# Edges as one transfer, K and V low halves on VectorE, three graph groups per key and value tile and 25 in the query stage, early query weight loads

## The reference, cut to what matters

```python
xn = layernorm(x)
# graph part: 41250 edges, W is 1024 x 1024, sparse, summed where edges repeat
W = zeros(1024, 1024).at[src, dst].add(edge_weight)        # indices over 1023 fall out
g = xn @ W.T + bias
# linear attention, 16 heads of 64
q, k, v = split(xn @ W_qkv)
q, k = relu(rmsnorm(q, qn_w)), relu(rmsnorm(k, kn_w))
kv = einsum('bhnd,bhne->bhde', k, v)
out = einsum('bhnd,bhde->bhne', q, kv) / (q . sum(k) + eps)
x = x + g + out @ W_out + b_out
# mixture of experts: 8 experts, the 2 best for each token
t = rmsnorm(layernorm(x)) * norm_scale
logits = t @ gate_w + gate_b
x = x + sum over the top 2 of softmax(top_v) * (swiglu(t @ w1[e] + b1[e]) @ w2[e] + b2[e])
```

## Time and profile before

| | |
|---|---|
| median of three runs | 1087.6 us |
| the profiled execution | 1086.58 us |
| its span in the profile | 1084.7 us |
| mean granted TensorE clock | 0.948 |
| busy: PE, DVE, ACT, POOL | 948.2, 731.1, 305.3, 186.7 us |

### The profile page before, as it was taken

The page is one execution under the profiler, slowest core; times in us unless marked ns, Lnnn a source line. Parts: engine busy times, 40 slices in busy tenths (PEclk is TensorE's granted clock), DMA queues, the critical chain, the costliest instruction groups (busy, mean ns, idle before and its releaser), DMA issues.

```text
span 1084.7 us, 16241 instructions
## 1 busy us (share of the span) xinstructions
PE 948.2 (87%) x5425; PEld 589.6 (54%) x5426; DVE 731.1 (67%) x1213; ACT 305.3 (28%) x520; POOL 186.7 (17%) x217
## 2 busy tenths in 40 slices
PE   3589899888899599999999999997828999999992
PEld 2346566666566366545656666665615445455551
DVE  4646888999888599715787778765264555555551
ACT  3525333233333111423212222222102333233321
POOL 1210000000000000000334333322201333333321
PEclk9789899999999699999999999998858999999997
DMA  8512566555455601395115555555618997977553
GB/s 255 187 59 78 174 191 197 185 181 159 143 169 173 215 21 40 85 290 170 40 39 145 156 164 170 173 160 168 214 47 300 326 264 192 312 198 192 119 100 58
DMA packets 90410, 176.49 MB, mean 163 GB/s; under 512 B 25235, under 2 KB 40537, under 8 KB 90337
## 3 DMA queue, kind: packets, MB, share of 16 engines
q1 hardware_dynamic: 82577, 147.40, 42.6%
q0 software_dynamic: 7776, 28.32, 11.7%
HBM read 113.54 MB, written 62.67 MB: 162 GB/s over the span
## 4 chain that ended last, share of the span: by engine, by line
PE 35%; DVE 31%; DMA 14%; ACT 6%; issue 5%; POOL 4%; SPq 3%; DVEq 1%; POOLq 0%; ACTq 0%
PE windows L1066 9%; PE bank L943 8%; DMA arena<-t_dram,arena 6%; DMA arena<-in_w_flat 5%; PE bank L1084 4%; DVE arena L1476 4%; DVE arena L1483 3%; DVE arena L1630 3%; PE bank L966 2%; PE bank L790 2%; PE bank L1057 2%; PE bank L972 2%; POOL arena L687 2%; DVE arena L1463 2%; DVE arena L1461 2%
## 5 line engine op out<-in xcount | busy, mean ns | idle before, releaser
L790 PE MATMUL bank<-arena 128*125 128x512 f16 x960 | 222.5, 390 | 31.7 <-POOL arena L656 18.4
L790 PEld LDWEIGHTS bank<-arena 128*125 128x125 f16 x960 | 132.6, 141 | 109.4 <-issue 27.7
L1066 PE MATMUL windows<-arena 128*128 x648 | 148.8, 379 | 0.0
L943 PE MATMUL bank<-arena 128*128 128x416 f16 (+1 forms) x576 | 110.0, 348 | 9.4 <-DMA arena<-split_dram 9.4
L966 PE MATMUL bank<-arena 128*125 128x512 f16 x432 | 99.2, 387 | 8.3 <-DVE arena L1666 6.8
L1066 PEld LDWEIGHTS windows<-arena 128*128 128x128 f16 x648 | 63.4, 98 | 65.1 <-issue 0.5
L972 PE MATMUL bank<-arena 128*125 128x512 f16 x432 | 95.8, 379 | 0.0
L943 PEld LDWEIGHTS bank<-arena 128*128 128x128 f16 x576 | 56.3, 99 | 56.1 <-DMA arena<-split_dram 10.0
L966 PEld LDWEIGHTS bank<-arena 128*125 128x125 f16 x432 | 60.1, 140 | 43.8 <-DVE arena L1666 7.2
L972 PEld LDWEIGHTS bank<-arena 128*125 128x125 f16 x432 | 59.0, 137 | 33.4
L1084 PE MATMUL bank<-arena 128*128 x324 | 74.3, 379 | 2.2 <-DVE arena L1838 2.2
(11 more groups left out here) (243 smaller groups left out, 1453.5 us busy)
## 6 DMA issues: line engine op xcount, KB each, us to landing
arena<-split_dram SPq DMA_DIRECT2D x56, 512.0 KB, 7.0
arena<-in_w_flat SPq DMA_DIRECT2D x44, 512.0 KB, 4.7
split_dram<-arena SPq DMA_DIRECT2D x88, 256.0 KB, 2.7
arena<-in_w_flat SPq DMA_DIRECT2D x40, 256.0 KB, 3.3
split_dram<-arena SPq DMA_DIRECT2D x80, 128.0 KB, 2.3
arena<-in_x SPq DMA_DIRECT2D x20, 448.0 KB
arena<-in_w_qkv SPq DMA_DIRECT2D x8, 1024.0 KB, 9.5
t_dram<-arena SPq DMA_DIRECT2D x10, 448.0 KB
```

Of the source, the lines that this page charges most:

```text
L790: mm = pe.matmul(bank[b][0:TT, :], xt[:, l, k, tok(i)], wkv[:, r, k, c0:c0 + 512], start=(k == 0 and n == 0), stop=(k == KT - 1 and n == 2))
L943: mm = pe.matmul(bank[u % 3][:, 0:n], wq[h][:, l, k, :], xt[:, r, k, a:a + n], start=(k == 0 and c == 0), stop=(k == KT - 1 and c == 2))
L1066: mm = pe.matmul(bank[6][:, :], rowT[s][:, l, k, :], arena16[:, bass.ds(off + (r * KT + k) * 512, 512)], start=(k == 0 and c == 0), stop=( ...
```

## The change

- **Edges.** The host lays `src`, `dst`, `edge_weight` (padded) and the two preceding `dst` of each row side by side, and one transfer loads all. POOL's four memsets and the semaphore ahead of them go. On SP, three weight parts now stand ahead of x of tile 1, and the edges behind it.
- **Low halves of the K and V weights.** All eight on DVE; the second ACT pass for parts 3, 5, 7 goes. Instructions of the start are put in another order on ACT and DVE, `window_picks` behind `v_half(0, ...)`.
- **Halves.** Tile 1 takes six, tiles 2 to 7 five, tiles 8 and 9 four (before: four in tile 1, five in 2 to 9).
- **Groups.** Three a tile (`KV_GROUPS` = 24): the fourth, behind `kv_unit(i, 1, 1536)` on PE and `v_half(i, 1)` on DVE, goes. The query stage has 25, on units 0 to 14, and the splits start at unit 15 (`FIRST_SPLIT`, before 11).
- **Query weights.** `load_wq(0, 0)` is issued at the end of tile 7, (0, 1) ahead of the store of the last half; (2, 1) and (3, 0) stand ahead of the writes of `w_acc`. The last `kv_sums` stands behind query unit 0.
- **Mix.** The quarters per tile are 6, 5, 5, 5, 5, 5, 5, 4 in place of 5, 5, 5, 5, 6, 6, 4, 4, and in tiles 8 and 9 `add_half` stands behind the third and the fourth quarter, not behind all.

```diff
-KV_GROUPS = 4 * (NT - 2)
+KV_GROUPS = 3 * (NT - 2)
...
-        HALVES_OF = [0, 4] + [5] * (NT - 2)
+        HALVES_OF = [0, 6, 5, 5, 5, 5, 5, 5, 4, 4]
...
-        for u in range(11):
-            if u in (1, 3, 5, 7, 9, 10):
+        for u in range(15):
+            if u % 3 > 0:
                 Q_AT[u, "mid"] = KV_GROUPS + len(Q_AT)
             Q_AT[u, "end"] = KV_GROUPS + len(Q_AT)
-        FIRST_SPLIT = 11
+        FIRST_SPLIT = 15
...
-        QUARTERS_OF = {2: 5, 3: 5, 4: 5, 5: 5, 6: 6, 7: 6, 8: 4, 9: 4}
+        QUARTERS_OF = {2: 6, 3: 5, 4: 5, 5: 5, 6: 5, 7: 5, 8: 5, 9: 4}
...
             load_wkv(0)
             load_wkv(1)
-            sp.wait_ge(edges_in, 1)
...
+            load_wkv(2)
             load_x(1)
+            sp.dma_start(edges_all, edges).then_inc(table_in, 16)
             sp.dma_start(knw, kn_w.partition_broadcast(P)).then_inc(knw_in, 16)
...
             for i in range(NT):
                 for n in halves(i):
+                    if n == 2 * EARLY - 1:
+                        sp.wait_ge(kv_mm, 4 * NT)
+                        load_wq(0, 1)
                     store(n)
                     if n + 2 < 2 * EARLY:
                         ask(n + 2)
...
+                if i == NT - 3:
+                    for h in range(2):
+                        sp.wait_ge(part_out[h], 32 * N_PIECE_Q)
+                    load_wq(0, 0)
...
             load_wq(2, 0)
+            load_wq(2, 1)
+            load_wq(3, 0)
             for k in range(KT):
                 sp.wait_ge(acc_lo, k + 1)
 ...
-                if k == 3:
-                    load_wq(2, 1)
-            load_wq(3, 0)
             sp.wait_ge(acc_out, 16 * 2 * KT)
             load_wo(1)
             load_wq(3, 1)
             load_wg()
...
-            for m in LO_ON_POOL:
-                pool.wait_ge(wkv_hi, m + 1)
-                pool.tensor_tensor(wkv_part(1, m), wide_part(m), wkv_part(0, m), ALU.subtract)
...
                 kv_unit(i, 1, 1536)
-                steps(n + 3, any_kv)
-            pe.wait_ge(v_lo, 2 * NT)
-            kv_sums()
...
+                    if first and u == 0:
+                        pe.wait_ge(v_lo, 2 * NT)
+                        kv_sums()
...
                 v_half(i, 1)
-                accumulate(n + 3)
-                piece_lo(hs[4])
+                for m in hs[4:]:
+                    piece_lo(m)
...
-                for q in quarters(i):
+                for q in quarters(i, 0, 3):
                     quarter_split(q)
-                for half in range(2):
-                    add_half(i, i % 2, half)
+                add_half(i, i % 2, 0)
+                for q in quarters(i, 3, 4):
+                    quarter_split(q)
+                add_half(i, i % 2, 1)
+                for q in quarters(i, 4):
+                    quarter_split(q)
```

More of the change, by code:

```diff
@@ L485, in _ @@
             ask(1)
[L486 to L490, removed]
-                if i + 5 < NT:
-                    load_x(i + 5)
             def load_wq(t, h):
@@ L508, in load_wg @@
                                      wg_dram[hl].rearrange("(k p c) -> p k c", p=P, c=D)[:, :, half * 512:half * 512 + 512]).then_inc(wg_in[half], 16)
-            for h in range(2):
-                sp.wait_ge(part_out[h], 32 * N_PIECE_Q)
-            load_wq(0, 0)
-            sp.wait_ge(kv_mm, 4 * NT)
-            load_wq(0, 1)
+            for i in range(NT):
+                for n in halves(i):
+                    if n == 2 * EARLY - 1:
+                        sp.wait_ge(kv_mm, 4 * NT)
+                        load_wq(0, 1)
+                    store(n)
+                    if n + 2 < 2 * EARLY:
+                        ask(n + 2)
+                if i + 5 < NT:
+                    load_x(i + 5)
+                if i == NT - 3:
+                    for h in range(2):
+                        sp.wait_ge(part_out[h], 32 * N_PIECE_Q)
+                    load_wq(0, 0)
             for h in range(2):
@@ L1505, in _ @@
             wkv_part_lo(0)
-            wkv_part_lo(1)
             for half in range(2):
                 xt_lo_half(0, half)
+            wkv_part_lo(1)
+            stats(1)
+            wkv_part_lo(2)
+            norm(1)
             window_counts()
-            wkv_part_lo(2)
-            stats(1)
-            wkv_part_lo(4)
-            norm(1)
-            window_picks()
+            for m in (3, 4):
+                wkv_part_lo(m)
             v.wait_ge(knw_in, 16)
             k_half(0, 0)
-            wkv_part_lo(6)
+            for m in (5, 6):
+                wkv_part_lo(m)
             k_half(0, 1)
+            wkv_part_lo(7)
             norm_of_k(0)
@@ L1525, in _ @@
                 v_half(0, c)
+            window_picks()
+            hs = halves(1)
+            for n in hs[0:2]:
+                piece_lo(n)
             v.wait_ge(kv_used, START + 1)
@@ L1530, in _ @@
             read_windows()
+            for n in hs[2:4]:
+                piece_lo(n)
             k_half(1, 1)
             norm_of_k(1)
+            for n in hs[4:6]:
+                piece_lo(n)
             read_keys()
             xt_lo_half(2, 0)
-            make(0, 0)
-            piece_lo(0)
+            make(0)
+            stats(3)
             v_half(1, 0)
-            stats(3)
             xt_lo_half(2, 1)
             norm(3)
-            piece_lo(1)
-            make(1, 1)
+            make(1)
             v_half(1, 1)
-            piece_lo(2)
-            piece_lo(3)
             v.wait_ge(acc_zero, KT)
             for i in range(2, NT):
-                n, hs = 4 * (i - 2), halves(i)
+                n, hs = 3 * (i - 2), halves(i)
                 v.wait_ge(kv_used, START + i)
```

138 lines of the change are left out of this document (63 added, 75 removed).

## The result

The changed kernel takes 1100.9 us (median of four runs, 1099.5 to 1101.4) against 1086.6 of before (four runs, 1085.4 to 1088.9). The ratio is 1.0133, with a 95% interval of 1.0111 to 1.0155: **slower by 14 us**, where I had forecast 1078 and gave 0.09 to slower. The profiled execution took 1100.75, its span is 1099.0.

| start of ... (us) | before | predicted | changed | the same, second profile |
|---|---|---|---|---|
| tile 2 on DVE | 111.0 | 95 | 99.6 | 102.2 |
| tile 9 on DVE | 334.2 | 315.8 | 334.4 | 327.8 |
| last group's add on DVE | 444.3 | 442.5 (its steps on PE done) | 464.1 | 457.6 |
| first `wo_fold` on PE | 481.9 | 475.7 | 498.8 | 493.1 |
| mix stage | 517.7 | 514.1 | 536.4 | 530.9 |

A forecast was written before the change was run, and what follows sets the result against it. PE and DVE were both nearly full in key and value tiles, PE in the query stage, where DVE would become just the bound. Gains of 3.5 before the mix and 6 in it gave 1078 us, range 1070 to 1085 (1058 to 1086 with rivals).

The forecast's parts named there:

- Key and value tiles: Tiles 2 to 8: dropping a group gains 0.2 us a tile in tiles 2 to 7, 2.4 together; bounds 0 and 11.
- Start: Before tile 2: part 7 done at about 46, tile 2 on DVE at 95, gain 16 us (12 or 19 otherwise).
- the slower rival: Start: pairs of halves at 13 us each give 1087; with no gain at the start 1094; chance 0.09.
- Into the query stage: Tile 9's first k_half to DVE's query groups: 30.3 us, at 346.1; PE no longer waits for query weights.
- Units 0 to 14: Query stage: DVE just the bound with 95 us against PE's 92; groups' last PE steps end at 442.5.
- Output weights: Query stage's end: weights land 29 us (27 to 32) after unit 15; PE stands 16 us before the first fold.
- Mix: Mix stage: PE's tile 9 waits less for add_half; gain 6 us (2 to 9).
- Sum: Whole kernel: 3.5 us gained up to the mix plus 6 in it, 9.5; 1077.1 profiled, 1078 as median.

The follow-up runs named there:

- second profile: The changed kernel run once more, nothing altered, with a profile: 1098.8 us (one run).
- tile1_four: The changed kernel with the halves as before, four in tile 1 and five in tiles 2 to 9: 1097.7 us, ratio 1.0091 to the kernel before.
- mix_alone: The kernel before with only the mix stage's edit (quarters per tile, add_half between quarters): 1081.6 us, ratio 0.9947.
- both moves together: The changed kernel with hs[2]'s low half and the second transpose's low half both moved earlier on DVE: 1084.7 us, ratio 0.9972 to the kernel before.

## Why the prediction was wrong

Two steps failed: **Key and value tiles**, which lost time where a small gain was forecast, and **Start**, which gained half of what was forecast. The first reads: "Without the group it is free at 202.86 and stands for 3.4 us. The cover is gone and the gain with it: 0.2 us a tile", with the bound "0, if each load lands later by 0.2". The wait is there as said (3.97), but the bound had no loss in it, and the tiles lose 0.2 to 2.3 us each. Tile 2 to tile 9 takes 234.8 and 225.7 us in the two profiles, 223.2 and 223.5 before, 220.8 predicted. Two things did it.

- A cover gone doesn't only end a gain. From then on each tenth that the load is late is paid: it took 5.0 us on average and up to 6.3 where ACT waited for it, and I had reckoned with one row of 4.72. Before, the group hid all up to 4.9.
- I wrote that PE "only waits longer for DVE's low half of the next tile", and named nobody whom that hurts. The wait grew from 1.50 to 2.85 us, and after it the granted clock was at its lower level for a unit in some executions (3 of 6, 6 of 6). The sum had no term for the clock, though the earlier trace rows showed the first unit after a 7.06 us wait at 7.1 us in place of 4.4, and I used just that row elsewhere.

The other steps against the two profiles of the changed kernel:

- **Start**: 4.6 and 7.2 us short. Eleven profiles with the six halves in tile 1 begin tile 2 at 97.1 to 105.2, mean 101.7, the four with the old start at 108.4 to 111.0, mean 109.7: the gain is 8, not 16. This is the larger miss in the second profile. Part 7 at 46 was right; the rounds of the pairs took 10.1 and 8.5 us, not 8.8 and 7.9, and PE's last two units in it 2.1 us longer after a wait of 5.48. tile1_four shows what the step had wrong: the third pair of halves costs tile 1 at least 6 us, and only without it does tile 2 begin at 95. The gain is near the 7 of the slower rival ("the start is not gained"), but the rounds are only 1.9 us longer in all, not 13 us each.
- **Into the query stage**: 30.2 us against 30.3, unit 0 without a wait. Right.
- **Units 0 to 14**: right in kind (DVE is the bound), 3.1 us too short: 99.5 against 96.4, in both profiles.
- **Output weights**: right. The wait of PE is 17.9 against 16; the fold comes 30.7 us after unit 15's end, against 29 (27 to 32). In all profiles it comes 33.7 to 37.6 us behind the last group's add, whatever else is changed: the stage ends by that chain.
- **Mix**: right as an edit (6.1 by itself). In company the stretch from the mix to the end is 562.7 and 566.1 us long, 567.0 and 569.9 before: 1 to 7 won. In each kernel with all the edits PE also has two to four waits for `add_half` of 0.8 to 1.8 us in other tiles, in mix_alone none above 0.8; where they come from wasn't tried.
- **Sum**: 4.6 (start) + 14.0 (tiles) + 4.5 (units and fold) - 0.8 (fold to mix) + 1.6 (mix to end) = 23.9 for the first profile; 7.2 + 4.9 + 5.3 - 0.5 + 5.0 = 21.9 for the second (23.8 and 21.8 without the rounding). The tiles are the largest term in the one only; in the other the four losses are of one size. All four are on the same side. The stated range ended at 1086 and left out the slower rival's own 1087 to 1094; the measured time lies above that too.

What I didn't put side by side is the simple question behind it: what does a group cost where it goes, and what where it comes from? 4.1 us (with the evacuations) against nothing in tiles 2 to 7 as changed, or 2.4 a tile at best. For 8 groups that is a loss of some 14 to 33 us, and the start, the query weights and the mix, 18 us together, don't pay for the loss as it came. It stays open why the runs of the changed kernel with more and with less of the lower clock (mean 0.938 and 0.953) take the same 1099.5 to 1101.4 us. In the two profiles the 9.1 us that the tiles of the first lose more are for the most part met by a start 2.5 and a stretch from mix to end 3.4 us shorter; whether by chance, two profiles can't tell.

## What to carry to other kernels

Before work is moved off a busy engine, ask what it covers: a load that was hidden by it is on the path afterwards with all its scatter, so the bound of such a term needs a loss. Price the moved piece at both ends, by the length of the chain and not by busy shares: PE looked full in the query stage and DVE free, yet the stage ended by the groups. And where two bounds lie within 1 us of each other, removing either alone shows little or nothing (5 and 0 us here); both moves together gave 17 us.

## What the hardware showed that I had not expected

The same wait of PE is followed by a fall of the granted clock in some executions and not in others. Ahead of the first unit of key and value tiles 3 to 9, over the profiles of all these kernels: after waits of 0.2 to 1.5 us none of 49 units was slow; after 1.56 none of 6; after 1.85 one of 3; after 2.2 three of 6; after 2.85 twenty-four of 36. A slow unit takes 6.9 to 7.1 or 8.4 us in place of 5.39: the lower level (1.2 GHz) lasts for a part or most of a unit, although PE is busy meanwhile. The units of 8.4 us come in rows: in three profiles they follow each other tile by tile to the last wait of 2.85 us (six, four and three of them); why is not shown. The Trainium skill (TensorE: Matmul & The Clock Gate, HAM oscillation — how this bites in real kernels) describes the pattern: a loop that waits once in each turn can pay the slow start of the clock in every turn. The first profile of the changed kernel agrees, with 8.36 us units in six tiles of six; the second, with three of six, shows that it needn't come each time.
